# Attention by recomputed scores: maxima first, key-by-query scores less the maximum, and fp32 values in four column groups

## The chip, the cores and the metric

The kernel runs on one core of one Trainium2 chip. The metric is device time in microseconds (us) for one launch, taken as the median of several runs; beside it stands one profiled execution of the same program. A core has five engines that run their own instruction streams: TensorE (PE in the profile, with its weight loads as PEld), VectorE (DVE), ScalarE (ACT), GpSimd (POOL) and SyncE (SP), which here only issues DMAs. They wait for each other by semaphores.

## What is computed

The input is eight sequences of 256 rows by 256 features, in fp32. Two layers follow, each an attention-like part and a feed-forward part, each wrapped in a normalisation before and after and a residual sum. Only the first attention matters here:

```python
B, S, H, nh, hd = 8, 256, 256, 16, 16
qkv = layernorm(x) @ w_qkv + b_qkv
q, k, v = split(qkv)                              # each B, S, 16 heads, 16 columns
scores = einsum('bqhd,bkhd->bhqk', q, k) / hd + slope[h] * (key - query)
scores = where(key <= query, scores, lowest)
attn = softmax(scores, axis=-1)
out = einsum('bhqk,bkhd->bqhd', attn, v)
x = x + layernorm(out @ w_proj + b_proj)
```

After it come a mixture of experts (64 experts, four for each row), a state-space layer and a dense feed-forward part. The change doesn't touch these.

## The kernel before

The program is a chain of stages, with a barrier of all engines after each: load of x, `stage_norm`, `stage_qkv`, `stage_attention`, then the stages of the experts, the state-space layer (`stage_ssm`) and the dense part.

**`stage_qkv`** goes through four chunks of 512 rows. For each chunk TensorE forms four blocks of queries and keys (six matmuls of 512 columns each, in `pq`) and then four tiles of values (six matmuls of 256 columns each, in `pv`, two banks). ScalarE adds the bias of a block; VectorE splits it into three bf16 parts (L401 to L404), whose sum is the fp32 value, and SyncE stores the parts to DRAM (`qk_parts`), two buffers in turn. For each tile of values VectorE runs five linked operations (L412 to L417) that add the bias and split into three bf16 parts in `vparts`. GpSimd sets all of `vparts` to one at the stage's start; VectorE's first work waits for loads.

**`stage_attention`** has 128 steps, one for each head of each sequence. The scores of a head are one bf16 matmul over 99 rows: six products of parts of queries and keys (96 rows) and three rows for the slope (alibi). These rows are the tile `stack`; SyncE fills it for one sequence by 24 DMAs of 64 KB (L498), with two sequences' room. In step n TensorE writes scores, query by key (L547 to L551; a triangular mask is added by a matmul with the identity); VectorE takes the maximum of each row with its sign turned (`negmax`, L642, L643); ScalarE takes the exponential with it as bias (L614, L615); two steps later TensorE turns the probabilities by fp32 transposes (L561), ScalarE and VectorE split the turned ones into two fp16 parts (`probT_hi` L623, `probT_lo` L648), and four steps later TensorE multiplies them by the parts of the values (15 matmuls of 16 or 17 columns, L574), where a column of ones yields the sum. Once for each sequence the output is divided, turned, projected (L595) and the bias is added (L667). After each sequence's loads SyncE issues the copy of its values (`vs`) and two DMAs of 1 MB that write zeros to `slots_in` in DRAM (16 in all), which the expert stage needs much later.

The order of each engine's work is written out by hand; the first two sequences' steps are unrolled and the others run in a loop of registers.

Of the kernel before, what the change touches and what calls it, by code (L numbers as in the profile page):

```python
# [13 lines left out]
P = 128  # L14
# [108 lines left out]
def stage_norm(chip, x, y, xh, xl, ident, add_y, make_norm, half=False, x_loaded=None, out=None, rows=None):  # L123
# [6 lines left out]
    with ExitStack() as ctx:  # L130
# [34 lines left out]
        with nc.Block() as block:  # L165
# [15 lines left out]
            def _(dve):  # L181
                link = linker(dve, chain)
                if x_loaded is not None:
                    dve.wait_ge(*x_loaded)

# [107 lines left out]
STACK = len(PAIRS) * HD + PARTS  # L293
VCOL = HD + 1 + 2 * HD
V_PARTS = ((0, HD + 1), (HD + 1, 2 * HD + 1), (2 * HD + 1, VCOL))


def stage_qkv(chip, xh, xl, vparts, qk_dram, ins):
# [3 lines left out]
    with ExitStack() as ctx:  # L302
# [10 lines left out]
        vwhole = sb("vwhole", [P, 2, D])  # L313
        vrest = sb("vrest", [P, D])
# [7 lines left out]
        v_done, v_link = chip.sem("v_done"), chip.sem("v_link")  # L322
        ones_set = chip.sem("ones_set")
        NB = 2 * KD
        with nc.Block() as block:
            @block.sync
            def _(sp):
# [3 lines left out]
                for c in range(NCH):  # L331
                    for blk in range(NB):
                        n = c * NB + blk
                        sp.wait_ge(qk_parts, n + 1)
                        sp.dma_start(qk_dram[blk // KD, blk % KD, :, :, c * CHUNK:(c + 1) * CHUNK],
                                     parts[:, n % 2, :, :]).then_inc(qk_stored[n % 2], 16)
                for s in range(2):
                    sp.wait_ge(qk_stored[s], NCH * NB // 2 * 16)

            @block.gpsimd  # L340
            def _(pool):
                chip.clear_old()
                nc.gpsimd.memset(vparts[:], 1.0).then_inc(ones_set, 1)

            @block.tensor
            def _(pe):
                pe.wait_ge(split_done, 2)
                for c in range(NCH):
# [10 lines left out]
                    for t in range(c * TPC, (c + 1) * TPC):  # L359
                        if t >= 2:  # L360

                            pe.wait_ge(v_link, 5 * (t - 1) - 4)
# [19 lines left out]
            def _(dve):  # L382
# [9 lines left out]
                vlink = linker(dve, v_link)  # L392
                dve.wait_ge(ones_set, 1)
                for c in range(NCH):
# [10 lines left out]
                    for t in range(c * TPC, (c + 1) * TPC):  # L405
                        dve.wait_ge(v_done, t + 1)
                        dst = [vparts[:, t, :, a:a + HD] for a, _ in V_PARTS]

                        def heads(ap):
                            return ap.rearrange("p (h c) -> p h c", c=HD)  # L410
# [9 lines left out]
SLOTS = 4  # L420
WORK = 4
LAG_T, LAG_LO, LAG_V = 2, 3, 4
S_NORM, S_TURN, S_PROJ = 3, 5, 6
U_TURN, U_PROJ, USES = 5, 7, NH + 2


def work_use(s):

    return s if s < U_TURN else s + 1 if s == U_TURN else s + 2


def stage_attention(chip, vparts, qk_dram, y, ident, xs, xs_clear, ins):
# [3 lines left out]
    STEPS = 2 * NH  # L436
    TURNS = B // 2
    LOADS = 2 * KD * len(PAIRS) + 1
    with ExitStack() as ctx:
# [4 lines left out]
        mask = sb("mask", [P, P], BF16)  # L444
        stack = sb("stack", [STACK, 2, 2, NH, S], BF16)
        vs = sb("vs", [P, 2, 2, NH, VCOL], BF16)
        negmax = sb("negmax", [P, SLOTS, 2])
        prob = sb("prob", [P, SLOTS, 3 * P])
        probT_hi = sb("probT_hi", [P, SLOTS, 3 * P], F16)
        probT_lo = sb("probT_lo", [P, SLOTS, 3 * P], F16)  # L450
        rsum = sb("rsum", [P, 2, NH])
        on = sb("on", [P, 2, D])
        oT = sb("oT", [P, KD, S])
        work = [pb(f"work{n}", [P, 512]) for n in range(WORK)]
        pturn = [pb(f"pturn{n}", [P, 512]) for n in range(2)]
        acc = [pb(f"acc{n}", [P, 512]) for n in range(2)]
        acc_h = [a[:, 0:NH * (HD + 1)].rearrange("p (h c) -> p h c", c=HD + 1) for a in acc]
        blank = sb("blank", [P, BLANK, D])
        blank_set = chip.sem("blank_set")
        loaded = chip.sem("loaded")  # L460
        in_loaded = [chip.sem("in_loaded") for _ in range(2)]
        scored, maxed, exped, p_turned = (chip.sem(n) for n in ("scored", "maxed", "exped", "p_turned"))
        hi_done, lo_done, pv_done = chip.sem("hi_done"), chip.sem("lo_done"), chip.sem("pv_done")
        inverted, normed, o_turned = chip.sem("inverted"), chip.sem("normed"), chip.sem("o_turned")
        o_copied, projected, y_ready = chip.sem("o_copied"), chip.sem("projected"), chip.sem("y_ready")

        def turns(eng, step):

            for st in range(STEPS):
                step(0, st, True, False)  # L470
            with eng.Fori(1, TURNS) as turn:
                for st in range(STEPS):
                    step(turn, st, False, False)
            for st in range(S_PROJ + 1):
                step(TURNS, st, False, True)

        def exists(h, first, tail):

            return not (first and h < 0) and not (tail and h >= 0)

        with nc.Block() as block:
            @block.sync
            def _(sp):
                for s in range(2):
                    sp.dma_start(stack[len(PAIRS) * HD:, s, :, :, :], ins["alibi"]).then_inc(loaded, 16)
                for dst, src in ((bproj, "bproj"), (identb, "identb"), (mask, "causal_add"), (wproj, "wproj")):
                    sp.dma_start(dst[:], ins[src]).then_inc(loaded, 16)

                def body(turn):
                    for s in range(2):  # L490

                        after(sp, scored, turn * STEPS - (1 - s) * NH)
                        for side in range(2):
                            for r, pair in enumerate(PAIRS):
                                for k in range(KD):
                                    src = qk_dram[side, k, :, pair[side], bass.ds(turn * (2 * S) + s * S, S)]
                                    half = slice(k * NH // KD, (k + 1) * NH // KD)
                                    sp.dma_start(stack[r * HD:(r + 1) * HD, s, side, half, :],  # L498
                                                 src.rearrange("(j c) l -> c j l", c=HD)).then_inc(in_loaded[s], 16)

                        after(sp, pv_done, turn * STEPS - (1 - s) * NH)
                        sp.dma_start(vs[:, s, :, :, :], vparts[:, bass.ds(turn * 4 + 2 * s, 2), :, :]
                                     ).then_inc(in_loaded[s], 16)
                        for part in range(BLANKS // B):
                            rows = bass.ds(turn * (2 * BLANKS // B) + s * (BLANKS // B) + part, 1)
                            sp.dma_start(xs.rearrange("(a p n) d -> a p (n d)", p=P, n=BLANK)[rows, :, :]
                                         .rearrange("a p n -> p (a n)"), flat(blank[:])).then_inc(xs_clear, 16)

                sp.wait_ge(blank_set, 1)
                body(0)  # L510
                with sp.Fori(1, TURNS) as turn:
                    body(turn)

            @block.gpsimd
            def _(pool):
                chip.clear_old()
                nc.gpsimd.memset(blank[:], 0.0).then_inc(blank_set, 1)

            @block.tensor
            def _(pe):  # L520
                pe.wait_ge(loaded, 6 * 16)

                def bank_free(turn, st, use, first, tail):

                    n = st // NH * USES + use - WORK
                    if (first and n < 0) or (tail and n >= 0):
                        return
                    q, old = n // USES, n % USES
                    if old not in (U_TURN, U_PROJ):
                        head = old if old < U_TURN else old - 1 if old < U_PROJ else old - 2  # L530
                        pe.wait_ge(exped, turn * STEPS + (q * NH + head + 1))
                    elif not (first and q == 0):

                        pe.wait_ge(o_copied if old == U_TURN else y_ready, turn * 2 + q)

                def bank(st, use):
# [1450 lines left out]
```

## Time and profile before

| | us |
|---|---|
| median of 3 runs | 1746.62 (1745.62 to 1748.82) |
| the profiled execution | 1745.03 |
| its span | 1743.2 |
| start of the qkv stage's first DMA | 33.15 |
| first DMA issue of the attention stage | 123.17 |
| first matmul of the attention stage | 146.12 |
| first work of the next stage | 345.63 |

Over the whole span TensorE is busy for 71% of the time, VectorE for 56%, ScalarE for 40% and GpSimd for 17%. A start time in a timeline is counted from the start of the span. A row of the timeline or of groups names line, engine, operation, output and inputs by the program's tile names, and then shapes; what stands in brackets is how long the engine had been idle before, and what released it. An fp32 matmul shows as two records in the trace, a bf16 one as one.

### The profile page before, as it was taken

The page shows a single profiled execution, that of the slowest core. Times are in us where ns is not written, and L with a number is a line of the kernel's source. Part 1 is how long each engine was busy: PE and PEld are TensorE (multiplying, and loading weights), DVE is VectorE, ACT ScalarE, POOL GpSimd, SP SyncE. Part 2 cuts the span into 40 slices and gives each one's busy share as a digit, 9 for nine tenths or more (in the row PEclk, how much of TensorE's full clock was granted, in tenths as well). Part 3 has the DMA queues.
Part 4 walks back from the last instruction along what each step waited for, and adds up shares of the span by engine and source line. Part 5 has one row for each costly group of instructions (what it writes and reads, how often), then busy time and mean ns, then how long its engine had stood idle before and what let it go on. Part 6 is the DMA issues. An engine that isn't in the chain of part 4 may idle for free. (4 is left out here: it accounts for less than half of the span.)

```text
span 1743.2 us, 27239 instructions
## 1 busy us (share of the span) xinstructions
PE 1244.2 (71%) x9461; PEld 1032.9 (59%) x9462; DVE 983.5 (56%) x2128; ACT 694.1 (40%) x1709; POOL 295.6 (17%) x311
## 2 busy tenths in 40 slices
PE   2645898735877777201574799899899989996294
PEld 1534777624767766100353688788788868875184
DVE  4874788755624544336564566566566656652535
ACT  3104777540222322003233455455455545541533
POOL 3000000022770000473000601300400230000201
PEclk9866999855998988655798899999999999998597
DMA  1239689011227988330221522322332222200101
GB/s 71 73 92 196 177 182 162 30 54 79 94 96 265 349 295 294 126 105 24 79 96 52 152 72 80 103 73 80 90 95 71 85 91 74 85 25 12 52 0 49
DMA packets 100745, 186.53 MB, mean 107 GB/s; under 512 B 13046, under 2 KB 53110, under 8 KB 98038
## 3 DMA queue, kind: packets, MB, share of 16 engines
q1 hardware_dynamic: 94492, 168.36, 32.0%
q0 software_dynamic: 6144, 16.79, 3.0%
q8 instruction: 60, 0.98, 0.2%
q14 instruction: 49, 0.40, 0.1%
HBM read 122.90 MB, written 58.98 MB: 104 GB/s over the span
## 5 line engine op out<-in xcount | busy, mean ns | idle before, releaser
L1648 ACT ACTIVATE decay<-masked,negcum 128x128 f32<-128x128 f32 x512 | 188.0, 391 | 296.9 <-DVE mixT L1674 288.5
L1674 DVE TENSOR_TENSOR mixT<-pcb,decay 128x384 f32<-128x384 f32 x256 | 130.6, 551 | 69.3 <-PE pcb L1596 67.7
L1697 DVE COPY cT<-pcT 128x512 f32<-128x512 f32 x128 | 88.2, 689 | 123.5 <-PE pcT L1583 123.5
L1594 PE MATMUL pcb<-cT,bT 128*128 128x256 f32 x512 | 155.2, 385 | 0.0
L274 PE MATMUL turned<-ident,xn 128*128 128x128 f32 x96 | 26.5, 435 | 166.3 <-ACT xn L234 141.6
L274 PEld LDWEIGHTS turned<-ident,xn 128*128 128x128 f32 x96 | 17.2, 217 | 175.1 <-ACT xn L234 147.2
L1583 PE MATMUL pbT<-xh,wh 128*128 128x512 f32 x256 | 112.0, 438 | 11.7 <-POOL wl L1556 10.6
L1663 DVE TENSOR_TENSOR masked<-cumrow,mask 128x512 f32<-128x512 f32 x128 | 90.0, 703 | 43.1 <-DMA cumrow<-ssm_cum 43.0
L1583 PE MATMUL pcT<-xh,wh 128*128 128x512 f32 x256 | 101.6, 397 | 15.0 <-DVE cT L1697 15.0
L1596 PEld LDWEIGHTS pcb<-cT,bT 128*128 128x128 f32 x512 | 98.1, 192 | 14.2
L1583 PE MATMUL pcT<-xh,wl 128*128 128x512 f32 x256 | 102.2, 399 | 0.0
L1583 PE MATMUL pbT<-xh,wl 128*128 128x512 f32 x256 | 101.8, 398 | 0.0
L1583 PE MATMUL pcT<-xl,wh 128*128 128x512 f32 x256 | 101.4, 396 | 0.0
L1583 PE MATMUL pbT<-xl,wh 128*128 128x512 f32 x256 | 101.3, 396 | 0.0
L1596 PE MATMUL pcb<-cT,bT 128*128 128x128 f32 x512 | 99.1, 276 | 0.0
L1648 ACT ACTIVATE decay<-masked,rest 128x128 f32<-128x128 f32 x256 | 99.1, 387 | 0.0
L1186 POOL DMA_INDIRECT back<-slots_out,slots x64 | 60.6, 946 | 210.2 <-PEq L1178 191.0
L1594 PEld LDWEIGHTS pcb<-cT,bT 128*128 128x128 f32 x512 | 89.0, 194 | 10.9
L1553 POOL TENSOR_TENSOR wh<-wraw,none 128x512 fp32r<-128x512 f32 x32 | 34.5, 1078 | 319.3 <-PE pcT L1583 317.1
L170 POOL MEMSET power<- 128x16 f32 x5 | 0.6, 111 | 501.7 <-SPq L165 398.8
L234 ACT ACTIVATE y<-y,shift,rstd 128x256 f32<-128x256 f32 x64 | 33.2, 589 | 124.5 <-POOL shift L177 124.4
L614 ACT ACTIVATE prob<-work,negmax 128x128 f32<-128x128 f32 x128 | 47.1, 368 | 81.3 <-DVE negmax L643 78.8
(251 smaller groups left out, 3408.6 us busy)
## 6 DMA issues: line engine op xcount, KB each, us to landing
cumrow<-ssm_cum SPq DMA_DIRECT2D x128, 256.0 KB, 3.3
slots_in<-blank SPq DMA_DIRECT2D x16, 1024.0 KB, 8.5
xg<-slots_in SPq DMA_DIRECT2D x32, 512.0 KB, 6.0
slots_out<-yg SPq DMA_DIRECT2D x32, 512.0 KB, 4.4
stack<-qk_parts SPq DMA_DIRECT2D x192, 64.0 KB, 3.9
wring<-in_expert_quads SPq DMA_DIRECT2D x16, 768.0 KB, 7.8
wring<-in_expert_w SPq DMA_DIRECT2D x64, 192.0 KB, 3.2
wraw<-in_w_bc SPq DMA_DIRECT2D x32, 256.0 KB, 2.7
```

The source lines that it names most:

```text
L234: return nc.scalar.activation(dst, src, ACT.Identity, bias=shift[:, norm, t:t + 1], scale=rstd[:, norm, t:t + 1])
L274: last = nc.tensor.transpose(turned[b % 2][:, k, t * P:(t + 1) * P], normal(b)[:, t, k * P:(k + 1) * P], ident[:])
L614: nc.scalar.activation(prob[:, r, 0:P], src[:, 0:P], ACT.Exp, bias=negmax[:, r, 0:1])
L1186: nc.gpsimd.indirect_dma_start(out=back[:, i % DEPTH, k, :], out_offset=None, in_=ys[:, :], in_offset=bass.IndirectOffsetOnAxis(slots[:, i ...
L1553: nc.gpsimd.tensor_tensor(wh[:, j, :], wraw[:, i % 2, :], none[:].broadcast_to([P, WCOL]), ALU.add).then_inc(w_half, 1)
L1583: last = nc.tensor.matmul(bank[:], w[:, j, col:col + P], a[:, k, c * CHUNK:(c + 1) * CHUNK], start=(m == 0), stop=(m == len(parts) - 1))
L1594: nc.tensor.matmul(pcb[n % 2][q][:, 0:S], bT[:, n % 2, o:o + P], cT[:, n % 2, o:o + S], start=True, stop=True)
L1596: last = nc.tensor.matmul(pcb[n % 2][q][:, S:REACH], bT[:, n % 2, o + P:o + S], cT[:, n % 2, o + P:o + S], start=True, stop=True)
L1648: last = nc.scalar.activation(decay[:, n % 2, q, lo:lo + P], masked[:, n % 2, q, lo:lo + P], ACT.Exp, bias=bias)
L1663: nc.vector.tensor_tensor(masked[:, n % 2, :, 0:S], row, mask[:].unsqueeze(1) .broadcast_to([P, BPC, S]), ALU.add)
L1674: last = nc.vector.tensor_tensor(mixT[:, n % KEEP, q, :], pcb[n % 2][q][:], decay[:, n % 2, q, :], ALU.mult)
L1697: nc.vector.tensor_copy(cT[:, n % 2, :], pcT[:]).then_inc(c_out, 1)
```

## The change

It rewrites the attention stage, and moves the zeroing of `slots_in`.

The scores are computed twice. The first pass is as before and only yields the maxima. They are kept for a unit, which is half of a sequence's heads (eight steps; 16 units). After a unit one transpose brings its 16 columns of maxima into 16 partitions (`turn`), VectorE splits them into three bf16 parts (`split`, four linked operations), and SyncE writes the parts by three DMAs into three further rows of `stack`, on the queries' side (`shift`); on the keys' side these rows are ones. The second pass, two units behind the first, multiplies over 102 rows, with keys as the rows of the result (`scores_turned`, four matmuls as in the first pass), so the maximum is already taken off, and ScalarE takes the exponential of all 384 columns at once and writes it in fp32. No probability is transposed or split. The values stay in fp32 (`vpad`, padded to 32 columns a head); for four heads at a time 16 fp32 matmuls write to four groups of 32 partitions, half of them with a tile of ones that yields the sum, so that the result is already turned; VectorE takes the reciprocal and multiplies.

`stack` has room for four units. All is unrolled. SyncE's order becomes load(0), load(1), load(2), shift(0), shift(1), and then load(u + 3), shift(u + 2) for u = 0, 1, ...; a load is now 12 DMAs of 64 KB for eight heads. The 16 zeroing DMAs take a tile of `y` as source: eight are issued at the start of the first norm stage and one after every second store of the qkv stage, which at its end waits for all of them.

```diff
 stage_norm:
+            if fill is not None:
+                @block.sync
+                def _(sp):
+                    for part in range(BLANKS // 2):
+                        fill(sp, part)
 stage_qkv:
+                        if n % 2:
+                            fill(sp, BLANKS // 2 + n // 2)
                 for s in range(2):
                     sp.wait_ge(qk_stored[s], NCH * NB // 2 * 16)
+                sp.wait_ge(*filled)
...
-                nc.gpsimd.memset(vparts[:], 1.0).then_inc(ones_set, 1)
+                nc.gpsimd.memset(vpad[:], 0.0).then_inc(zeros_set, 1)
...
-                        vlink(nc.vector.tensor_tensor(vwhole[:, t % 2, :], pv[t % 2][:], bv[:], ALU.add))
-                        vlink(nc.vector.tensor_copy(dst[0], heads(vwhole[:, t % 2, :])))
-                        vlink(nc.vector.tensor_tensor(heads(vrest[:]), heads(vwhole[:, t % 2, :]), dst[0],
-                                                      ALU.subtract))
-                        vlink(nc.vector.tensor_copy(dst[1], heads(vrest[:])))
-                        vlink(nc.vector.tensor_tensor(dst[2], heads(vrest[:]), dst[1], ALU.subtract))
+                        for odd in range(2):
+                            at = odd * (VW + HD)
+                            last = nc.vector.tensor_tensor(pairs[:, :, at:at + HD], heads(pv[t % 2][:], odd),
+                                                           heads(bv[:], odd), ALU.add)
+                        last.then_inc(v_out, 1)
 stage_attention, SyncE:
+                def load(u):
+                    seq, k = u // 2, u % 2
+                    if u >= ROOM:
+                        sp.wait_ge(turned, (u - ROOM + 1) * HALF)
+                    for side in range(2):
+                        for r, pair in enumerate(PAIRS):
+                            src = qk_dram[side, k, :, pair[side], seq * S:(seq + 1) * S]
+                            sp.dma_start(stack[r * HD:(r + 1) * HD, u % ROOM, side, :, :],
+                                         src.rearrange("(j c) l -> c j l", c=HD)).then_inc(in_loaded[u % ROOM], 16)
+                def shift(u):
+                    sp.wait_ge(max_split, u + 1)
+                    for part in range(PARTS):
+                        row = stack[SHIFT + part:SHIFT + part + 1, u % ROOM, 0, :, :]
+                        sp.dma_start(row.rearrange("p j (t l) -> p (j t) l", l=P),
+                                     short[:, part, :]).then_inc(shift_loaded[u % 2], 16)
...
+                load(0)
+                for dst, src in ((identb, "identb"), (mask, "causal_add")):
+                    sp.dma_start(dst[:], ins[src]).then_inc(loaded, 16)
+                load(1)
+                load(2)
+                for dst, src in ((bproj, "bproj"), (wproj, "wproj")):
+                    sp.dma_start(dst[:], ins[src]).then_inc(loaded, 16)
+                for u in range(LEAD):
+                    shift(u)
+                for u in range(UNITS):
+                    if u + 3 < UNITS:
+                        load(u + 3)
+                    if u + LEAD < UNITS:
+                        shift(u + LEAD)
 TensorE:
+                pe.wait_ge(loaded, (ROOM + 4) * 16)
+                pe.wait_ge(ones_set, 2)
+                def scores(n):
+                    u, h = head(n)
+                    if n % HALF == 0:
+                        pe.wait_ge(in_loaded[u % ROOM], (u // ROOM + 1) * LOADS * 16)
+                    if n >= S_BANKS:
+                        pe.wait_ge(maxed, n - S_BANKS + 1)
...
+                def scores_turned(n):
+                    u, h = head(n)
+                    if n % HALF == 0:
+                        pe.wait_ge(shift_loaded[u % 2], (u // 2 + 1) * PARTS * 16)
+                    if n >= T_BANKS:
+                        pe.wait_ge(exped, n - T_BANKS + 1)
...
+                def values(n):
+                    u, odd = n // HALF, n % HALF // QUADS
+                    seq, k = u // 2, u % 2
+                    pe.wait_ge(exped, n + 1)
+                    if not odd and u >= 2:
+                        pe.wait_ge(normed, u - 1)
+                    for m, (lo, col) in enumerate(((0, 0), (P, S))):
+                        for side in range(2):
+                            for g in range(QUADS):
+                                h = k * HALF + 2 * g + odd
+                                left_side = (vpad[:, 2 * seq + m, h * VW:(h + 1) * VW], ones[:, odd, :])[side]
+                                last = nc.tensor.matmul(
+                                    po[u % 2][g * VW:(g + 1) * VW, side, lo:S], left_side,
+                                    probT[:, (n - QUADS + 1 + g) % HELD, col:col + S - lo],
+                                    start=(not odd and m == 0 and side == 0), stop=(odd == 1 and m == 1),
+                                    skip_group_check=True)
+                    last.then_inc(pv_done, 1)
...
+                for i in range(-LEAD * HALF, STEPS + HALF):
+                    n = i + LEAD * HALF
+                    if n < STEPS:
+                        scores(n)
+                    if 0 <= i < STEPS:
+                        scores_turned(i)
+                    if n % HALF == AT_TURN and 0 < n <= STEPS:
+                        turn(n // HALF - 1)
+                    if i - LAG_PV >= 0 and (i - LAG_PV) % QUADS == QUADS - 1 and i - LAG_PV < STEPS:
+                        values(i - LAG_PV)
+                    if i % HALF == AT_PROJ and i >= 2 * HALF and i // HALF % 2 == 0:
+                        project(i // HALF // 2 - 1)
 VectorE:
+                    if n < STEPS:
+                        maxima(n)
+                    if n % HALF == AT_SPLIT and HALF <= n <= STEPS + 1:
+                        split(n // HALF - 1)
+                    if i % HALF == AT_NORM and i >= HALF:
+                        normalise(i // HALF - 1)
```

The constants are HALF = 8 steps in a unit, LEAD = 2 units, ROOM = 4 units, AT_TURN = 0, AT_SPLIT = 1, AT_NORM = 3, AT_PROJ = 5, S_BANKS = 2, T_BANKS = 3 and LAG_PV = 2.

## Rows read from the trace of the kernel before

**Rows 1.** Windows: us, then busy time by engine, TensorE clock, DMA share, GB/s.

```profile
50.70:68.70 18.00, 12.82 (x55) 10.72 (x55) 16.11 (x36) 3.35 (x5) 0.00 (x0) 0.81 0.26 89
...
123.17:146.10 22.93, 0.00 (x0) 0.01 (x1) 0.00 (x0) 0.00 (x0) 1.80 (x1) 0.50 1.08 142
146.10:340.00 193.90, 171.54 (x2904) 143.49 (x2904) 153.44 (x423) 144.28 (x391) 0.00 (x0) 0.95 0.69 155
```

**Rows 2.** Timeline at the start of the qkv stage: start us, us, engine, line.

```profile
33.25 10.55 POOL L343 MEMSET vparts<- 128x12544 bf16 x1 [5.50 <-POOLq L165]
37.68 6.96 DVE L387 CAST wh<-wraw 128x1536 fp32r<-128x1536 f32 x1
...
50.73 0.43 DVE L401 CAST parts<-whole 128x512 bf16<-128x512 f32 x1 [4.30 <-ACT whole L378]
```

**Rows 3.** Timeline of VectorE in a qkv chunk: a block's split, then a tile of values.

```profile
76.30 0.42 DVE L401 CAST parts<-whole 128x512 bf16<-128x512 f32 x1
...
78.55 0.42 DVE L412 TENSOR_TENSOR vwhole<-pv,bv 128x256 f32<-128x256 f32 x1
...
80.58 0.42 DVE L412 TENSOR_TENSOR vwhole<-pv,bv 128x256 f32<-128x256 f32 x1
```

**Rows 4.** Timeline of TensorE in the qkv stage: a block, tiles, a late tile.

```profile
69.27 0.39 PE L355 MATMUL pq<-xh,wh 128*128 128x512 f32 x1
...
70.63 0.28 PE L365 MATMUL pv<-wh,xh 128*128 128x256 f32 x1
...
71.34 0.28 PE L365 MATMUL pv<-wh,xh 128*128 128x256 f32 x1
...
79.03 0.58 PE L365 MATMUL pv<-wh,xh 128*128 128x256 f32 x1 [6.81 <-DVE vwhole L412]
```

**Rows 5.** Memsets by group: count, then busy us, mean ns.

```profile
L1545 POOL MEMSET y<- 128x4096 f32 x1 | 3.5, 3511 | 0.0
```

**Rows 6.** Windows: DMA with two zeroing transfers at the end of a turn's loads.

```profile
302.00:307.00 5.00, 4.75 (x90) 3.89 (x88) 4.51 (x13) 4.27 (x13) 0.00 (x0) 1.00 0.99 381
```

**Rows 7.** Timeline of the attention stage's start: first loads, first matmul.

```profile
125.67 11.31 SPq L498 DMA_DIRECT2D stack<-qk_parts  x24
...
146.12 0.27 PE L547 MATMUL work<-stack 99*128 99x128 bf16 x1 [27.40 <-DMA vs<-vparts]
```

**Rows 8.** Later loads of `stack`: first load at 263.35, 11th and 12th, then all 24 from 216.33.

```profile
263.35 11.57 SPq L498 DMA_DIRECT2D stack<-qk_parts  x24
...
DMA to landing us min/median/max: 2.4/2.4/2.4
...
DMA to landing us min/median/max: 4.0/4.1/4.2
...
DMA to landing us min/median/max: 2.4/3.4/3.9
```

**Rows 9.** Timeline of one attention step at full clock.

```profile
201.15 0.22 PE L547 MATMUL work<-stack 99*128 99x128 bf16 x1
...
201.44 0.49 PE L561 MATMUL pturn<-ident,prob 128*128 128x128 f32 x3
...
201.64 0.29 DVE L642 TENSOR_REDUCE negmax<-work 128x1 f32<-128x128 f32 x1 [0.57 <-PE work L551]
...
201.85 0.41 DVE L643 TENSOR_REDUCE negmax<-work 128x1 f32<-128x256 f32 x1
```

**Rows 10.** Timeline of the state-space stage: 16 fp32 matmuls in four column groups.

```profile
1312.01 1.51 PE L1612 MATMUL py<-mixT,y 128*32 128x256 f32 x32
1313.45 0.50 PE L1583 MATMUL pbT<-xh,wh 128*128 128x512 f32 x1
```

**Rows 11.** Groups of the attention stage: busy us, mean ns, idle before.

```profile
L623 ACT ACTIVATE probT_hi<-pturn 128x384 f16<-128x384 f32 x128 | 62.9, 491 | 1.0 <-PE pturn L561 1.0
...
L595 PE MATMUL work<-wproj,oT 128*128 128x256 f32 x64 | 17.6, 422 | 0.7 <-ACT oT L629 0.7
...
L657 DVE RECIPROCAL rsum<-acc 128x16 f32<-128x16 f32 x16 | 2.9, 221 | 0.7 <-PE acc L574 0.7
```

More of the change, by code:

```diff
@@ L120, with stage_norm @@
 NORM_SEQS = B // NORM_GROUPS
-def stage_norm(chip, x, y, xh, xl, ident, add_y, make_norm, half=False, x_loaded=None, out=None, rows=None):
+def stage_norm(chip, x, y, xh, xl, ident, add_y, make_norm, half=False, out=None, rows=None, fill=None):
     nc = chip.nc
@@ L463, in stage_attention @@
[L463 to L475, printed above, removed]
@@ L477, in exists @@
-        def exists(h, first, tail):
-            return not (first and h < 0) and not (tail and h >= 0)
+        mask = sb("mask", [P, 2, P], BF16)
+        stack = sb("stack", [STACK, ROOM, 2, HALF, S], BF16)
+        ones = sb("ones", [P, 2, VW])
+        negmax = sb("negmax", [P, 2, HALF, 2])
+        short = sb("short", [2 * HALF, PARTS, P], BF16)
+        left = sb("left", [2 * HALF, P])
+        probT = sb("probT", [P, HELD, 3 * P])
+        rinv = sb("rinv", [P, S])
+        oT = sb("oT", [P, 2, KD, S])
@@ L483, in _ @@
             def _(sp):
-                for s in range(2):
-                    sp.dma_start(stack[len(PAIRS) * HD:, s, :, :, :], ins["alibi"]).then_inc(loaded, 16)
-                for dst, src in ((bproj, "bproj"), (identb, "identb"), (mask, "causal_add"), (wproj, "wproj")):
-                    sp.dma_start(dst[:], ins[src]).then_inc(loaded, 16)
[L489 to L507, printed above, removed]
@@ new lines, in shift @@
+                def shift(u):
[4 more added lines that the diff above has]
+                                     short[:, part, :]).then_inc(shift_loaded[u % 2], 16)
+                for u in range(ROOM):
+                    sp.dma_start(stack[ALIBI:, u, :, :, :], ins["alibi"][:, :, u % 2 * HALF:(u % 2 + 1) * HALF, :]
+                                 ).then_inc(loaded, 16)
@@ L516, in _ @@
                 chip.clear_old()
-                nc.gpsimd.memset(blank[:], 0.0).then_inc(blank_set, 1)
+                nc.gpsimd.memset(ones[:], 0.0).then_inc(ones_set, 1)
+                pool.wait_ge(ones_set, 1)
+                for odd in range(2):
+                    last = nc.gpsimd.memset(ones[:, odd, odd * HD:(odd + 1) * HD], 1.0)
+                last.then_inc(ones_set, 1)
             @block.tensor
             def _(pe):
[L521 to L534, printed above, removed]
@@ L600, in _ @@
-                turns(pe, step)
-            def bank(st, use):
-                return work[(st // NH * USES + use) % WORK]
+                pe.wait_ge(loaded, (ROOM + 4) * 16)
[6 more added lines that the diff above has]
+                        pe.wait_ge(maxed, n - S_BANKS + 1)
+                    q, k = (stack[0:SHIFT, u % ROOM, side, h, :] for side in range(2))
+                    dst = ps[n % S_BANKS]
+                    nc.tensor.matmul(dst[:, 0:P], q[:, 0:P], k[:, 0:P], start=True, stop=False)
+                    nc.tensor.matmul(dst[:, 0:P], identb[:], mask[:, 0, :], start=False, stop=True)
+                    nc.tensor.matmul(dst[:, P:3 * P], q[:, P:S], k, start=True, stop=False, skip_group_check=True)
+                    nc.tensor.matmul(dst[:, 2 * P:3 * P], identb[:], mask[:, 0, :], start=False, stop=True,
+                                     skip_group_check=True).then_inc(scored, 1)
@@ new lines, in scores_turned @@
+                def scores_turned(n):
[4 more added lines that the diff above has]
+                        pe.wait_ge(exped, n - T_BANKS + 1)
+                    q, k = (stack[:, u % ROOM, side, h, :] for side in range(2))
+                    dst = pst[n % T_BANKS]
+                    nc.tensor.matmul(dst[:, 0:S], k[:, 0:P], q, start=True, stop=False, skip_group_check=True)
+                    nc.tensor.matmul(dst[:, 0:P], identb[:], mask[:, 1, :], start=False, stop=True,
+                                     skip_group_check=True)
+                    nc.tensor.matmul(dst[:, S:3 * P], k[:, P:S], q[:, P:S], start=True, stop=False,
+                                     skip_group_check=True)
+                    nc.tensor.matmul(dst[:, S:3 * P], identb[:], mask[:, 1, :], start=False, stop=True,
+                                     skip_group_check=True).then_inc(turned, 1)
@@ new lines, in turn, with project @@
+                def turn(u):
+                    pe.wait_ge(maxed, (u + 1) * HALF)
+                    if u:
+                        pe.wait_ge(max_split, u)
+                    seq = (u - 4) // 2
+                    if seq >= 0:
+                        pe.wait_ge(y_ready, seq + 1)
+                    nc.tensor.transpose(misc[0:2 * HALF, 0:P], negmax[:, u % 2, :, :].rearrange("p j t -> p (j t)"),
+                                        ident[:]).then_inc(max_turned, 1)
+                def project(seq):
+                    pe.wait_ge(normed, 2 * seq + 2)
+                    pe.wait_ge(max_split, min(2 * seq + 4, UNITS))
+                    for t in range(2):
+                        for k in range(KD):
+                            last = nc.tensor.matmul(misc[:, t * D:(t + 1) * D], oT[:, seq % 2, k, t * P:(t + 1) * P],
+                                                    wproj[:, k, :], start=(k == 0), stop=(k == KD - 1),
+                                                    skip_group_check=True)
+                    last.then_inc(projected, 1)
@@ new lines, in _ @@
+                dve.wait_ge(loaded, (ROOM + 4) * 16)
+                for i in range(-LEAD * HALF, STEPS + HALF):
+                    n = i + LEAD * HALF
+                    if n < STEPS:
[4 more added lines that the diff above has]
+                        normalise(i // HALF - 1)
+                    if i % HALF == AT_ADD and i >= 2 * HALF and i // HALF % 2 == 0:
+                        add(i // HALF // 2 - 1)
@@ L1870, in program, with fill, _ @@
         x_loaded = chip.kept_sem("x_loaded")
+        blank_set = chip.kept_sem("blank_set")
+        blank = y[:, 0:BLANK, :]
+        def fill(sp, part):
+            rows = xs.rearrange("(a p n) d -> a p (n d)", p=P, n=BLANK)
+            sp.dma_start(rows[part, :, :], flat(blank)).then_inc(xs_clear, 16)
         with nc.Block() as block:
+            @block.gpsimd
+            def _(pool):
+                nc.gpsimd.memset(blank, 0.0).then_inc(blank_set, 1)
             @block.sync
```

257 lines of the change are left out of this document (85 added, 172 removed).

## The prediction

> **What bounds the kernel now.** I read the windows by stage first, then the timeline of each stage that the change touches, then the DMA issues. The program is a chain of stages with barriers, so a stage's length adds to the total, and only the span from 33 us to 345.63 us can change: the first norm stage, the qkv stage and the attention stage. In the qkv stage VectorE is busy for 16.11 of 18.0 us of a chunk and TensorE for 12.82 [rows 1], so VectorE sets the pace. In the attention stage two stretches differ. For 22.93 us no engine computes: all wait for the first sequence's loads [rows 1, 7]. Then for 193.90 us TensorE is busy for 171.54, at 0.95 of the full clock, VectorE for 153.44 and ScalarE for 144.28 [rows 1]: 128 steps at 1.51 us, TensorE first. There SyncE's loads are hidden, since the room for a sequence is asked for 16 steps (24 us) ahead and 24 loads need about 17 us (11.57 us of issues and at most 5.6 us from the last issue to its landing, by the growth seen in [rows 8]).
>
> **The qkv stage.** Its start: VectorE's cast of the weights began at 37.68 and lasted 6.96 us, that is, until just after GpSimd's memset ended (33.25 + 10.55 = 43.80) [rows 2]; the memset held it. The new one sets 8192 fp32 columns; at 3.511 us for 4096 [rows 5] that is 7.0 us, a gain of 3.5 us. But the weights' load now stands behind 8 MB of zeros, issued from about 9 us on. Zeros move at about 381 GB/s [rows 6], so they are done at 9 + 1 + 22 = 32 us at best and 39 us at 280 GB/s, which would hand the weights over some 2 us later than the memset would. I take 3.0 us of gain, bounds 3.5 and 0.
>
> Its chunks: a block's split takes 2.25 us and a tile's five operations 2.03 us [rows 3]. The split stays. The tile keeps two unlinked operations on 128 columns; by the maxima of 128 columns, whose follower starts 0.21 us later and which take 0.29 us [rows 9], 0.5 us. The floor of a chunk on VectorE is thus 4 x 2.25 + 4 x 0.5 = 11.0 us against 18.0. It isn't reached, since TensorE is no longer ahead. A block takes it 70.63 - 69.27 = 1.36 us and a tile 0.71 us [rows 4], with two banks for tiles: tiles three and four of a chunk are only formed after VectorE freed a bank, at 0.7 us each plus 0.2 us to be seen, 0.8 us more than VectorE's own 1.0 for both; and the next chunk's first block starts after the fourth tile: 1.36, about 0.65 for ScalarE's pass (0.49 for 384 columns [rows 11]) and 0.2 of latency, less 0.5, leave VectorE idle for 1.7 us. A store of 0.39 MB and a zeroing transfer of 1 MB need about 3.8 us at 381 GB/s, and two buffers come round in 4.5 us; I put 0.7 us a chunk on that wait. TensorE runs below full clock for part of the time (0.81 now [rows 1], after idle times such as 6.81 us [rows 4]), 0.4 us more. Sum 14.6 us, times four, less the 1.7 that has no follower: 56.7 against 72 us, a gain of 15.3. At the end the last zeroing transfer, issued some 3 us before VectorE's last tile, lands about 3 us after it: 3.0 lost. **The attention stage starts 3.0 + 15.3 - 3.0 = 15.3 us earlier**; with TensorE always at the lower clock (16.6 us a chunk) it would be some 8 us, with fewer waits 19.
>
> **The attention stage, step by step of TensorE.** The four score matmuls take 201.44 - 201.15 = 0.29 us [rows 9], and the second pass has the same columns: 0.29. The values are 16 fp32 matmuls for four heads, eight of 256 columns and eight of 128, each with 32 columns of weights, and the state-space stage runs just that: 1.44 us [rows 10], 0.36 a step. One projection for 16 steps: 64 records of 0.422 us that overlap, eight of them about 1.6 us, 0.1 a step. Sum 1.05 us a step, 8.4 a unit, against 1.51. ScalarE has one pass, about 0.5 us [rows 11]; VectorE's maxima take 0.21 + 0.41 = 0.62 us [rows 9]. The reciprocal of 256 columns isn't in the trace; it lies between 0.42 us (any 256-column operation, [rows 3]) and 16 times the 0.221 us of 16 columns [rows 11], 3.5 us. With 1.2 for the split, 0.42 and 0.35 for product and sum, VectorE has 7.4 to 10.5 us a unit. If compute set the pace, a unit would take 8.4 to 10.5 us.
>
> On column groups the Trainium skill says (TensorEngine Tiling (Array Packing), Key Properties) that a change of the tiling mode drains TensorE. The price of 1.44 us is from start to start of the neighbours [rows 10], so one drain at each end is in it, and the sum of the next paragraph doesn't move. Were two drains of one 0.22 us matmul to come on top of each of the 32 calls, it would be 14 us of work, all of it in the idle time found below.
>
> **The loads set the pace instead.** SyncE's order is load(3), shift(2), load(4), shift(3), ...: load(k+1) is queued behind shift(k-1), whose wait is for the split of unit k-1, which VectorE does after the maxima of step 8k+1; and those scores need load(k). So there is one ring from load(k) landed to load(k+1) landed, whatever room `stack` has. Its length:
> - from landing to the end of the maxima of step 8k+1: TensorE does two score blocks, one second-pass block and the transpose, 0.29 x 3 + 0.1 + 0.3 to be seen, then 0.62: 1.9 us at full clock, 2.7 us at half;
> - the split, four linked operations on 128 columns: 4 x 0.29 = 1.2 us;
> - three shift issues: a static issue takes 11.31 / 24 = 0.47 us [rows 7], so 1.4 us;
> - twelve loads: the twelfth is issued 11 x 0.47 = 5.2 us after the first and lands 4.2 us later (the first lands after 2.4, the twelfth after 4.0 to 4.2, in the row for them [rows 8]): 9.4 us.
>
> That is 13.9 us at full clock and 14.7 at half. TensorE works 8.4 of it and then idles for 5, and after such idle times it starts at the lower clock [rows 1, 4], so I take **14.3 us a unit**. VectorE's 7.4 to 10.5 us are covered.
>
> The stage then adds up:
> - first issue to first matmul: now 36 loads and `wproj` stand before it, as the wait for `loaded` covers the last issues. 24 loads were landed 21.8 us after the stage's start; 24 issued in 11.57 us land over 14.7 us (a landing time that grows from 2.4 to about 5.6), 0.61 us each. So 1.2 + 2 + 36 x 0.61 + 1.8 for the others: 27.0 us, against 22.95;
> - to load(3) landed: ten steps at VectorE's 0.62 and 0.3, split 1.2: 7.7; shift 1.4 and 2.4 to land: 11.5; scores, maxima and split of unit 1: 3; shifts 1.4; loads 9.4: 25.0 us;
> - twelve rings to load(15): 171.6 us;
> - the last 24 steps: eight at 1.1, sixteen without first-pass scores at 0.7, a projection and 1.5 for the clock: 23; exponential, values, reciprocal, product, projection and sum at the end, 5.9: 28.9 us.
>
> Sum 252.5 us against 345.63 - 123.17 = 222.5: 30.0 us more. With 15.3 us from the stage before it the change costs 14.7 us: 1745.03 + 14.7 = 1759.7 us; the profiled execution is 1.6 us under the median of the runs, so I say **1760**. Nothing after the stage changes: the zeros are needed no earlier.
>
> **The rivals.**
> - *The ring is short enough* (the other side). If twelve loads land with 2.4 us each instead of a growing time, a load takes 5.2 + 2.4 = 7.6 us, and with shift issues of 0.35 us and full clock the ring is 11.8 us; 12 x 2.5 less is 30 us, so 1730. For it: a turn whose loads came out slower had 3.4 us in the median [rows 8], and nothing else uses the queues now. Against it: even alone the landing time grows to 4.2 [rows 8]. It decides below 14.3 - 14.7 / 12 = 13.1 us a unit. Were the ring under 9 us, compute would bound it and the time would be about 1697.
> - *TensorE is the bound.* If the column groups didn't overlap, values would cost four times as much, 5.8 us for four heads, 2.4 us a step, 19 us a unit, 1817 us. Always at half clock a unit is 16.8 us: 12 x 2.5 more, 1790. Against both: [rows 10], and a TensorE without idle time ran at full clock [rows 1].
> - *The zeroing isn't free.* If each transfer took 5 us, eight would hold the weights until 53 us instead of 41, and the qkv stage's stores would wait: 1760 + 12 = 1772. That would mean the move costs what it should save. Against it: 381 GB/s [rows 6].
>
> **How the numbers follow.** The ring as worked out has a chance of 0.68; by itself it ranges from 1745 (13.4 us a unit and 18 us gained before) to 1778 (15.3 us, 12 gained). The short ring has 0.22, TensorE 0.06, the zeroing 0.04. A measurement of this kernel tells about 0.2%, 3.5 us, from no change. Faster is the short ring but for its upper end, and little of the main case: 0.22; the same 0.07; slower 0.71. The range, 1728 to 1780, leaves out the compute-bound end and most of TensorE's.
>
> **What would show it.** TensorE idle for some 5 us in each unit before a first-pass score, released by a load of `stack`; a period of 14.3 us between the first scores of units; SyncE issuing without pause from the split on; the first matmul 27 us after the stage's first issue; values at 1.44 us for four heads; the stage's start near 108 us; VectorE's chunks at 14.6 us. The prediction falls if units follow each other in under 13 us, or if TensorE has no such idle time.

## The result and the profile after

The changed kernel takes 1754.2 us in the median of 9 runs (1751.75 to 1763.26), the kernel before 1744.78 us (9 runs). The ratio is 1.0056, with a 95% interval of 1.004 to 1.0073: slower by about 10 us, where 14.7 were forecast. The profiled execution took 1751.75 us, with a span of 1750.0 against 1743.2.

The windows of the profile after, cut at the same events as the prediction's stretches (first split of the qkv stage, first DMA issue of the attention stage, its first matmul, load(3) landed, load(15) landed, start of the next stage):

```profile
47.18:111.84 64.66, 39.33 (x183) 34.17 (x181) 42.23 (x96) 10.32 (x15) 0.00 (x0) 0.81 0.61 228
111.84:136.89 25.05, 0.00 (x0) 0.01 (x1) 0.00 (x0) 0.00 (x0) 0.31 (x3) 0.50 0.53 122
136.89:163.94 27.05, 18.39 (x162) 12.39 (x163) 15.86 (x56) 3.92 (x8) 0.00 (x0) 0.63 0.11 31
163.94:324.67 160.73, 126.17 (x1597) 93.39 (x1597) 96.36 (x270) 47.05 (x96) 0.00 (x0) 0.85 0.22 61
324.67:354.27 29.60, 24.90 (x370) 18.12 (x370) 16.73 (x35) 10.58 (x24) 0.00 (x0) 1.00 0.01 3
```

The attention stage begins 11.3 us earlier than before (111.84 against 123.17), lasts 242.4 us against 222.5, and so the next stage begins 8.6 us later, at 354.27 against 345.63. The longest stretch is the fourth: 12 units in 160.73 us, 13.4 us each. In it TensorE is busy for 126 of 161 us at a mean clock of 0.85, VectorE for 96 and ScalarE for 47; nothing that computes fills it.

One unit of it, in the timeline (load(9) landed, first pass, split, shift issues, load issues, and then load(10) landed):

```profile
246.54 0.23 PE L533 MATMUL ps<-stack 99*128 99x128 bf16 x1 [1.53 <-DMA stack<-qk_parts]
...
249.12 0.28 DVE L637 TENSOR_TENSOR short<-left,short 16x128 bf16<-16x128 f32 x1
...
249.43 1.90 SPq L490 DMA_DIRECT2D stack<-short  x3
...
251.70 5.61 SPq L483 DMA_DIRECT2D stack<-qk_parts  x12
...
259.47 0.29 PE L533 MATMUL ps<-stack 99*128 99x128 bf16 x1 [4.42 <-DMA stack<-qk_parts]
```

This is the ring: 2.9 us from the load's landing to the last operation of the split, 2.3 us for three shift issues, 7.8 us for twelve loads and the last one's landing; then TensorE, idle for 4.42 us, goes on. The list of waits from 155 to 340 us names it (who waited for whom, total, times, longest):

```profile
DVE negmax L625 <- PE ps L536: 70.5, 41, 6.5
...
PE ps L533 <- DMA stack<-qk_parts: 37.9, 13, 6.2
```

Thirteen waits, one for each of load(3) to load(15). VectorE, above it in the list, waits behind TensorE.

### The profile page after: what moved, and what is told of

It reads as the page before. It is cut to its first block and busy times, and to the rows that moved or that the text cites. A ratio compares the mean times of both kernels' runs of the same rounds, so it can differ in the third digit from the quotient of the medians.

```text
span 1750.0 us, 24427 instructions
## 1 busy us (share of the span) xinstructions
PE 1237.1 (71%) x8677; PEld 1011.1 (58%) x8678; DVE 931.5 (53%) x2016; ACT 610.7 (35%) x1445; POOL 291.7 (17%) x314
## 5 line engine op out<-in xcount | busy, mean ns | idle before, releaser
L612 ACT ACTIVATE probT<-pst 128x384 f32<-128x384 f32 x128 | 61.6, 491 | 184.9 <-PE pst L552 179.8
L1587 PEld LDWEIGHTS pcb<-cT,bT 128*128 128x128 f32 x512 | 88.5, 193 | 10.9
L625 DVE TENSOR_REDUCE negmax<-ps 128x1 f32<-128x128 f32 x128 | 36.9, 288 | 101.7 <-PE ps L536 101.1
```

The source lines that it names most:

```text
L612: nc.scalar.activation(probT[:, n % HELD, :], pst[n % T_BANKS][:, 0:3 * P], ACT.Exp).then_inc(exped, 1)
L625: nc.vector.tensor_reduce(negmax[:, u % 2, j, 0:1], src[:, 0:P], AX.X, ALU.max, negate=True)
L1587: nc.tensor.matmul(pcb[n % 2][q][:, 0:S], bT[:, n % 2, o:o + P], cT[:, n % 2, o:o + S], start=True, stop=True)
```

## The experiments

**The loads a place earlier in the queue.** load(3) is issued before shift(0), and load(u + 4) before shift(u + 2). `stack` has the room; a load still waits until its place is free.

```diff
+                load(3)
                 for u in range(LEAD):
                     shift(u)
                 for u in range(UNITS):
-                    if u + 3 < UNITS:
-                        load(u + 3)
+                    if u + 4 < UNITS:
+                        load(u + 4)
                     if u + LEAD < UNITS:
                         shift(u + LEAD)
```

> SyncE's order becomes load(3) at the start and then load(u + 4) before shift(u + 2); nothing else changes. Theory (a ring from load to scores to split to shift to load sets the unit's length): the ring is cut, a unit falls from 13.3 us to 9.5 to 10.5 us, bounded by compute and SyncE's 7.6 us of issues, and the wait of TensorE for the loads (37.9 us in 13 places) all but goes; about 1706 us. Rival 1 (compute, at the lower clock, is what a unit takes): no change, 1754 us. Rival 2 (the transfers themselves are too slow): the wait for the loads stays, 1750 us or more.

Measured: 1703.09 us, ratio to the kernel before 0.9765 (0.9737 to 0.9793). SyncE's timeline:

```profile
187.44 6.91 SPq L483 DMA_DIRECT2D stack<-qk_parts  x12
194.40 1.78 SPq L490 DMA_DIRECT2D stack<-short  x3
197.77 6.31 SPq L483 DMA_DIRECT2D stack<-qk_parts  x12
204.12 1.77 SPq L490 DMA_DIRECT2D stack<-short  x3
206.69 6.67 SPq L483 DMA_DIRECT2D stack<-qk_parts  x12
```

Loads now follow each other every 9.6 us (187.44 to 206.69 for two), and from 190 to 208 us TensorE is busy for 17.22 of 18.00 us at full clock. In its list of waits no wait of a matmul for a load is left. The order of the issues is worth 51 us (some 45 of it, by an estimate, in twelve units of 9.6 us instead of 13.4). Compute was not what a unit took before, and the transfers were quick enough.

**The shift on another queue.** GpSimd, idle in this stage, issues the three shift DMAs; SyncE's loads then wait only for room.

```diff
@block.gpsimd
+                for u in range(UNITS):
+                    pool.wait_ge(max_split, u + 1)
+                    for part in range(PARTS):
+                        row = stack[SHIFT + part:SHIFT + part + 1, u % ROOM, 0, :, :]
+                        pool.dma_start(row.rearrange("p j (t l) -> p (j t) l", l=P),
+                                       short[:, part, :]).then_inc(shift_loaded[u % 2], 16)
@block.sync
-                for u in range(LEAD):
-                    shift(u)
-                for u in range(UNITS):
-                    if u + 3 < UNITS:
-                        load(u + 3)
-                    if u + LEAD < UNITS:
-                        shift(u + LEAD)
+                for u in range(3, UNITS):
+                    load(u)
```

> The changed kernel with the three shift DMAs of a unit issued by GpSimd instead of SyncE; the loads stay in order on SyncE and wait only for room. Theory (ring by queue order): the ring is cut here too, 1704 to 1712 us, depending on what an issue by GpSimd costs. Rival 1 (compute) and rival 2 (transfers): 1750 us or more.

Measured: 1697.74 us, ratio 0.9743 (0.9713 to 0.9772), a little better than forecast. GpSimd's timeline shows a unit every 9.3 us (189.12 to 207.77 for two) and 0.48 us for an issue:

```profile
189.12 1.44 POOL L511 DMA_DIRECT2D stack<-short  x3 [7.01 <-DVE short L631]
199.32 1.44 POOL L511 DMA_DIRECT2D stack<-short  x3 [8.77 <-DVE short L631]
207.77 1.44 POOL L511 DMA_DIRECT2D stack<-short  x3 [7.01 <-DVE short L631]
```

Two ways of cutting the same link, one by order and one by queue, give nearly the same time. The cost lay in the link.

**Half of the loads.** From unit 4 on, half of the loads of a unit are left out, so that half of the rows of `stack` keep an earlier unit's values; the order of the queue is that of the change.

```diff
                         for r, pair in enumerate(PAIRS):
+                            if u >= 4 and r >= len(PAIRS) // 2:
+                                continue
```

> The changed kernel, but from unit 4 on only six of the twelve loads are issued, so that half of the rows of stack are stale (work left out). Theory: the ring keeps its order and gets shorter by six issues of 0.48 us, 2.9 us a unit, from 13.3 to 10.4 us; twelve rings make 35 us, about 1720 us. Compute as rival: no change. If it were the transfers' bandwidth, half the bytes would give more than 35 us.

TensorE's wait counts six landings for such a unit. Measured: 1721.61 us, ratio 0.9865 (0.983 to 0.9899), 33 us less than the changed kernel. SyncE's shifts are now 10.2 us apart in the mean of twelve units (10.1 in the rows shown, 231.79 to 252.01 for two), and TensorE still waits for loads (8 waits, 15.8 us in all):

```profile
231.79 2.11 SPq L492 DMA_DIRECT2D stack<-short  x3
233.94 2.95 SPq L485 DMA_DIRECT2D stack<-qk_parts  x6
241.81 1.77 SPq L492 DMA_DIRECT2D stack<-short  x3
243.62 2.95 SPq L485 DMA_DIRECT2D stack<-qk_parts  x6
252.01 1.79 SPq L492 DMA_DIRECT2D stack<-short  x3
```

The ring shrinks by about what the issues took: in the mean of twelve units the issues of a load go from 6.1 to 3.1 us, and the ring from 13.4 to 10.2. Half the loads are also half the bytes, and this run doesn't part the two; that the bytes weren't the limit is shown by the two runs before, with all of the loads and shorter units.

**The zeroing moved, and nothing else.** The kernel before, with only the fill of the norm and qkv stages and its source in `y`; the two zeroing transfers for each sequence in the attention stage are gone.

```diff
-                        for part in range(BLANKS // B):
-                            rows = bass.ds(turn * (2 * BLANKS // B) + s * (BLANKS // B) + part, 1)
-                            sp.dma_start(xs.rearrange("(a p n) d -> a p (n d)", p=P, n=BLANK)[rows, :, :]
-                                         .rearrange("a p n -> p (a n)"), flat(blank[:])).then_inc(xs_clear, 16)
```

> The kernel before with only the zeroing moved to the norm and qkv stages. Theory (the move is nearly free): the last transfer and the stores' waits cost 3 to 5 us at the end of the qkv stage, and the attention stage gains some 2 us, since its second sequence's loads no longer share the queues with 1 MB transfers; 1744 to 1749 us. Rival (the zeroing holds up the weights and the stores): 1757 us or more.

Measured: 1739.51 us (12 runs), ratio 0.9969 (0.9952 to 0.9986): faster by 5 us, below what the theory had given it. The qkv stage pays nothing (the attention stage starts at 123.28, against 123.17). The gain is in the attention stage: from its first matmul to the next stage it takes 194.4 us (147.39 to 341.77), against 199.5 before. The 24 loads of the second sequence are issued in 13.08 us instead of 16.46, now that no 2 MB of zeros stand before them, but in neither profile does a matmul after the first wait for a load, so this isn't what the time shows. What only the kernel before has is a stop of TensorE, with no wait that the profile names, while the second sequence's 2 MB of zeros are moved (from 163 to 167 us the queues move 410 GB/s):

```profile
166.17 0.28 PE L549 MATMUL work<-stack 99*128 99x256 bf16 x1 [2.06 <-issue]
```

From 160 to 180 us its clock is 0.91 in the mean, against 1.00 with the zeroing moved, and its trace has 283 records of matmuls against 324. The stop and the lower clock fit most of the gain; why TensorE stopped is not shown.

The next stage starts at 341.77 instead of 345.63. So this part of the change by itself gains about 0.3%, and the rewrite of attention and values, if the two simply add, costs about 0.9%.

**Four banks for value tiles.** In the qkv stage `pv` has four banks, so that TensorE can form all tiles of a chunk without waiting for VectorE.

```diff
-        pv = [pb(f"pv{n}", [P, D]) for n in range(2)]
+        pv = [pb(f"pv{n}", [P, D]) for n in range(4)]
...
-                        if t >= 2:
-                            pe.wait_ge(v_out, t - 1)
+                        if t >= 4:
+                            pe.wait_ge(v_out, t - 3)
```

> The changed kernel with four banks instead of two for the value tiles of the qkv stage. Theory (the qkv chunks were mis-sized, since TensorE idles 5 to 6 us for a bank and then forms the late tiles and the next block at the lower clock): a chunk falls from 16 us to 11.5 to 12.5 us, TensorE's clock in the stage rises, and the kernel gets 12 to 17 us faster, 1738 to 1742 us. Rival (the stores behind 1 MB of zeros hold VectorE): a chunk stays above 15 us and the waits for the landing of parts grow by what the tiles lose; no more than 4 us faster.

Measured: 1742.74 us (10 runs), ratio to the kernel before 0.999 (0.9973 to 1.0007), and so some 11 us less than the changed kernel. The window from the first split to the attention stage's first issue is 51.74 us, against 64.66 us:

```profile
47.18:98.92 51.74, 32.75 (x182) 26.91 (x180) 41.26 (x96) 10.32 (x15) 0.00 (x0) 0.89 0.76 285
```

The same number of matmuls (182 records against 183) is 32.75 us of busy time at a clock of 0.89, against 39.33 us at 0.81. In the second chunk VectorE idles only for 0.7 us, for the landing of a store (in the fourth for 2.0); it takes 11.4 us (59.18 to 70.55):

```profile
59.18 0.41 DVE L403 CAST parts<-whole 128x512 bf16<-128x512 f32 x1
...
68.96 1.67 DVE L416 TENSOR_TENSOR vpad<-pv,bv 128x128 f32<-128x128 f32 x8
70.55 0.41 DVE L403 CAST parts<-whole 128x512 bf16<-128x512 f32 x1
```

**The attention stage's start.** `bproj` and `wproj` count on a semaphore of their own, and only the first projection and its sum wait for it.

```diff
-                    sp.dma_start(dst[:], ins[src]).then_inc(loaded, 16)
+                    sp.dma_start(dst[:], ins[src]).then_inc(proj_loaded, 16)
...
-                pe.wait_ge(loaded, (ROOM + 4) * 16)
+                pe.wait_ge(loaded, (ROOM + 2) * 16)
...
-                dve.wait_ge(loaded, (ROOM + 4) * 16)
```

> The changed kernel in which TensorE and VectorE no longer wait at the attention stage's start for bproj and wproj, and so not for the loads of units 1 and 2. Theory: the first matmul comes about 12 us after the stage's first issue instead of 25, but shift(0) still stands behind load(2) and the two issues after it, about 22 us after the first issue, against 34 us now; so 10 to 12 us faster, 1742 to 1744 us, and the ring is still 13.3 us. Rival (the stage's start is covered by the ring, which only begins with load(3)): less than 4 us.

Measured: 1743.73 us (10 runs), ratio to the kernel before 0.9989 (0.9968 to 1.001), some 10 us less than the changed kernel. The first matmul comes 13.1 us after the stage's first issue (112.89), and the shifts 22.6 us after it:

```profile
126.03 0.29 PE L534 MATMUL ps<-stack 99*128 99x128 bf16 x1 [15.61 <-DMA mask<-in_causal_add]
```

```profile
135.51 8.53 SPq L491 DMA_DIRECT2D stack<-short  x6
144.08 6.98 SPq L484 DMA_DIRECT2D stack<-qk_parts  x12
```

load(3) is landed 40.2 us after the stage's first issue, against 52.1. In this profiled execution (1746.53 us, above the median) the twelve rings then took 13.7 us each, not 13.4, and the rest 3.2 us more, so that the stage is only 5.5 us shorter; the ten runs are the better measure.

**All three together.** The shift on GpSimd's queue, the start, and four banks.

> The shift DMAs on GpSimd's queue, the start without the wait for bproj and wproj, and four banks for value tiles, all in one. Theory (three separate stretches, so the gains add up): 1698 less 12 to 17 less 10 to 13, 1668 to 1676 us. If they overlap: above 1680 us.

Measured: 1676.12 us (1675.63 to 1677.69), ratio 0.9605 (0.958 to 0.9631). The gains add up nearly in full, and this version beats both kernels. Over 165 us of its attention stage TensorE is busy for 151.76 us at a clock of 0.94:

```profile
115.00:280.00 165.00, 151.76 (x2122) 114.93 (x2120) 127.90 (x360) 61.56 (x128) 23.28 (x48) 0.94 0.27 74
```

**The wait for the zeroing later.** As the last one, with the wait moved from the end of the qkv stage to VectorE's first write of `y` in the attention stage.

```diff
-                sp.wait_ge(*filled)
...
+                        dve.wait_ge(*filled)
```

> As the kernel with all three, but the wait for the zeroing transfers stands before VectorE's first write to y in the attention stage instead of at the end of the qkv stage. Theory: the last transfer landed 1.9 us after VectorE's last tile, so 1 to 3 us less than that kernel, unless the attention stage's first loads queue behind the transfer, and then 0.

Measured: 1676.38 us, ratio 0.9605 (0.9574 to 0.9636): no difference from the kernel without it. The second case named, the loads queueing behind the transfer, isn't what the profiles show: the attention stage's first issue comes at 97.47 us instead of 100.14, its first matmul at 110.17 instead of 113.98, and the next stage starts at 275.17 instead of 280.01. The later stages, whose code is the same, took 5.8 us more in this execution (1401.7 against 1395.9). With four runs from 1673.53 to 1679.84 us and an interval of 5 us to either side, 1 to 3 us can't be told from none.

## Why the prediction was right, point by point

The direction and the mechanism held. That units are tied by a ring of load, scores, split, shift and load is shown three times: cut by order, cut by queue, and shortened by half of the loads. The rivals fell with it. The short ring (below 13.1 us a unit) did not occur in the mean, but it was close: the twelve rings took 12.6 to 14.6 us, five of them under 13.1. TensorE was not the bound, since cutting the link brought the unit down to 9.3 us. The zeroing was, in the kernel before, not a cost but a gain.

The terms, forecast against measured:

| term | forecast, us | measured, us |
|---|---|---|
| gain of the memset | 3.0 | 3.55 (first split at 47.18 against 50.73) |
| attention stage starts earlier by | 15.3 | 11.3 |
| first issue to first matmul | 27.0 | 25.05 |
| to load(3) landed | 25.0 | 27.05 |
| twelve rings | 171.6 | 160.73 |
| the rest | 28.9 | 29.6 |
| sum of the change until the next stage | +14.7 | +8.6 |

Part of the nearness is luck: the rings took 10.9 us less than forecast and the stage began 4.0 us later than forecast, and the two misses work against each other in the sum.

*The ring* was forecast at 14.3 us and measured at 13.4. The term that was mis-sized is the twelfth load's landing: 4.2 us in the row taken [rows 8], 2.5 to 2.6 us here. In the unit shown the last issue began at about 256.9 us and landed 2.5 us later. Why the loads land sooner stays open. Against that stood the shift issues, of 0.6 us instead of 0.47, and in the first four of the twelve rings the load issues: one of each twelve took 1.3 to 1.6 us instead of 0.43, so that they took 6.5 to 6.9 us together, not 5.8, and these rings 13.7 to 14.6 us. What held that issue is not shown. The first part of the ring, 2.9 us plus the wake of SyncE, was as forecast at full clock (1.9 + 1.2). Where TensorE had been idle for 4.42 us, the next unit's same part took 3.7 us (259.47 to the shifts at 263.21, at a granted clock of 0.50), against 2.9 (246.54 to 249.43, at 1.00): the half clock that the prediction counted on. The same part took 3.7 us in four of the twelve rings and 2.9 to 3.1 us in the other eight. TensorE idled for 2.9 us a unit on average (37.9 us in 13 waits), not 5: the ring was shorter, and its own work took 10.5 us of it (126.17 us in twelve) at a mean clock of 0.85, where 8.4 at full clock was counted.

*The qkv stage* was the larger miss in share: 11.3 against 15.3 us. The step that failed is the 0.4 us a chunk for the lower clock. VectorE's 9.0 us for the blocks and the 0.7 us for the stores were right, but TensorE stood idle for some 5.6 us in each chunk for a bank and then formed the late tiles and the next block's first matmuls at the lower clock, so the tiles took 4.0 us, not 2.8, and the gap before the next chunk was 2.4 us, not 1.7. The timeline of the second chunk:

```profile
72.54 0.88 DVE L416 TENSOR_TENSOR vpad<-pv,bv 128x128 f32<-128x128 f32 x4
73.08 0.58 PE L368 MATMUL pv<-wh,xh 128*128 128x256 f32 x1 [5.57 <-DVE vpad L416]
...
76.04 0.49 DVE L416 TENSOR_TENSOR vpad<-pv,bv 128x128 f32<-128x128 f32 x2 [0.79 <-PE pv L368]
...
78.96 0.43 DVE L403 CAST parts<-whole 128x512 bf16<-128x512 f32 x1 [2.43 <-ACT whole L381]
```

The kernel with four banks, in which that idle time is gone, took 12.9 us off the stage.

*The zeroing* was priced only where it arrived (3.0 us at the end of the qkv stage), and at nothing where it left, without a reason. In the kernel before, moving it gained 5 us; how much of that is in the changed kernel, no run shows. At the qkv stage's end the last transfer cost less than the 3.0: VectorE's last tile ended at 109.90 and the next issue came at 111.84, 1.9 us later, where the kernel before needs 0.5 us (122.66 to 123.17). That makes about 1.4 us, an estimate.

*Covered costs* were covered: the reciprocal, bounded at 0.42 to 3.5 us, took 1.75 us and delayed nothing.

Values for four heads took 1.44 us (247.89 to 249.33 in the unit shown), the very price of [rows 10]. By the rule on draining that the prediction cited from the Trainium skill (TensorEngine Tiling (Array Packing), Key Properties), the trace shows no charge beyond that price.

Two sums of the prediction don't come out of their terms. For the rival without overlap, values at four times the price make 0.29 + 0.29 + 1.44 + 0.1 = 2.1 us a step and 17 us a unit, so about 1792 us, not 2.4, 19 and 1817. And the terms up to load(3) landed, 11.5 + 3 + 1.4 + 9.4, make 25.3 us, not 25.0. Neither changes the forecast's direction.

What stays open: up to the next stage the profile shows 8.6 us, over the whole span 6.8 us, and the runs give about 10 us. The later stages' code is the same; they were 1.8 us shorter in the one profiled execution. Over the ten kernels' profiled executions they took 1392.5 to 1401.7 us, so 1.8 us is well within their scatter, and the changed kernel's runs scatter over 11 us.

## What to carry to other kernels

Write out the order of each DMA queue and ask of every wait in it what that wait needs, and whether something queued behind it is among the causes: here each load stood behind a small transfer that waited for the work on the load before it, so room for more loads bought nothing. A rewrite that makes the compute shorter needs a new look at how early its inputs are asked for. And ask where bulk transfers that nobody waits for disturb least: moving them was worth 0.3% here, hidden inside a slower whole.

## What the runs showed of the hardware

- The landing time of the same 64 KB loads in 512-byte rows, issued 0.48 us apart, differs between the two kernels. In the kernel before, 24 in a loop went from 2.4 to 5.6 us [rows 8], and the 24 unrolled ones at the stage's start (125.67) took 5.1 to 8.4 us. In the changed kernel the twelve of a unit took about 2.5 us, and 24 in a row at its start (121.81) 2.1 to 2.7 us. So neither the loop nor the length of the burst explains it by itself; the DMA engines' share of busy time differs too (51% at 133 GB/s for these last 24, 89% at 107 GB/s for those of [rows 8]), and the cause is open.
- An issue for 16 rows of 256 bytes into one partition took 0.6 us on SyncE, more than the 0.43 us for 64 KB, and 0.48 us on GpSimd.
- The reciprocal of 256 columns took 1.75 us and of 16 columns 0.22 us: 6.4 us for a thousand columns more, against about 1.05 for a sum of two tensors (0.69 us for 512 columns, 0.42 for 256).
- Eight 1 MB transfers of zeros ran one after another at about 390 to 450 GB/s and were done before the next stage's load of weights was issued.
